# One-core perceiver layer pair: context turned by VectorE's block transposes, value products in fours, softmax maximum terms on GpSimd, ones rows by DMA

## The reference

```python
# layer 0: 4 heads of 64; mask of 128 x 12544; keys and values from one product
kv = (context @ Wkv)
attn = softmax(where(mask, q @ k.T * 64**-0.5, -inf))
out = attn @ v
...
# layer 1: 16 heads of 16, no mask
q = x_1 @ Wq.T + bq
k = x_2 @ Wk.T + bk
v = x_2 @ Wv.T + bv
out = softmax(q @ k.T * 16**-0.5) @ v
```

## Time and profile before

| | us |
|---|---|
| median of three runs (1105.54 to 1106.64) | 1106.38 |
| the profiled execution's own time | 1106.16 |
| its span in the trace | 1104.5 |
| PE busy | 1018.3 (92%) |
| DVE busy | 524.3 (47%) |
| ACT busy | 547.1 (50%) |
| POOL busy | 274.5 (25%) |

### The profile page before, as it was taken

The page is one execution under the profiler, slowest core; times in us unless marked ns, Lnnn a source line. Parts: engine busy times, 40 slices in busy tenths (PEclk is TensorE's granted clock), DMA queues, the critical chain, the costliest instruction groups (busy, mean ns, idle before and its releaser), DMA issues. The chain is left out here.

```text
span 1104.5 us, 22373 instructions
## 1 busy us (share of the span) xinstructions
PE 1018.3 (92%) x8536; PEld 587.8 (53%) x8536; DVE 524.3 (47%) x1094; ACT 547.1 (50%) x1252; POOL 274.5 (25%) x326
## 2 busy tenths in 40 slices
PE   7999999999999999999969987489999999999976
PEld 4445554554555455455457974125555555555653
DVE  2223232322323232232144443888878888787525
ACT  2544454454445445444547622116666666666752
POOL 4444253334425333442403610600000000000000
PEclk9999999999999999999989997559999999999988
DMA  4434625342363334233200006655556666555200
GB/s 146 155 140 170 232 95 194 118 159 84 113 228 116 135 117 163 83 109 131 104 35 1 1 1 186 177 139 139 140 142 175 169 171 178 139 140 152 67 1 6
DMA packets 65132, 136.79 MB, mean 124 GB/s; under 512 B 12584, under 2 KB 46912, under 8 KB 62368
## 3 DMA queue, kind: packets, MB, share of 16 engines
q1 hardware_dynamic: 65056, 135.72, 40.1%
HBM read 81.88 MB, written 53.26 MB: 122 GB/s over the span
## 5 line engine op out<-in xcount | busy, mean ns | idle before, releaser
L1724 DVE TENSOR_REDUCE mx<-bank 128x1 f32<-128x896 f32 x224 | 245.1, 1141 | 58.8 <-PE bank L1608 57.8
L1806 ACT ACTIVATE p<-bank 128x512 f32<-128x512 f32 x392 | 212.6, 595 | 115.7 <-PE bank L1651 114.9
L504 PE MATMUL bank<-Wv,ctxT 128*128 128x512 f32 x392 | 180.2, 600 | 0.0
L1608 PE MATMUL bank<-krows,qrows 96*128 96x512 bf16 x448 | 129.0, 377 | 27.4 <-DVE mx L1724 19.5
L1664 PE MATMUL bank<-p,v 128*32 128x128 f32 x3136 | 127.0, 279 | 5.5 <-ACT p L1806 5.1
L1651 PE MATMUL bank<-qrows,krows 99*128 99x128 bf16 x1568 | 122.6, 222 | 0.0
L577 DVE CUSTOM_DVE_ANT_0 sc<-bank,pen 128x448 f32<-128x448 f32 x112 | 65.7, 620 | 104.7 <-issue 104.7
L1664 PEld LDWEIGHTS bank<-p,v 128*32 128x32 f32 x3136 | 74.3, 109 | 71.6 <-issue 43.8
L1651 PEld LDWEIGHTS bank<-qrows,krows 99*128 99x128 bf16 x1568 | 89.1, 98 | 39.2 <-issue 35.7
L504 PEld LDWEIGHTS bank<-Wv,ctxT 128*128 128x128 f32 x392 | 70.1, 190 | 73.5 <-issue 72.5
L379 POOL CAST kt<-kf 128x512 bf16<-128x512 f32 (+1 forms) x56 | 31.1, 556 | 309.4 <-ACT kf L663 309.4
(11 more groups left out here) (287 smaller groups left out, 1263.2 us busy)
## 6 DMA issues: line engine op xcount, KB each, us to landing
krows<-kscr SPq DMA_DIRECT2D x14, 1536.0 KB, 10.2
krows<-kscr SPq DMA_DIRECT2D x14, 1152.0 KB, 11.4
vscr<-v1s SPq DMA_DIRECT2D x14, 1004.5 KB, 3.9
v<-vscr SPq DMA_DIRECT2D x14, 1004.5 KB, 11.1
ctx<-ctx SPq DMA_DIRECT2D x14, 896.0 KB, 6.4
kscr<-kt SPq DMA_DIRECT2D x14, 768.0 KB, 3.6
kscr<-kt SPq DMA_DIRECT2D x14, 576.0 KB, 3.0
kscr<-kt SPq DMA_DIRECT2D x14, 512.0 KB, 4.5
```

What stands on the lines that cost most here:

```text
L504: ins = pe.matmul(bank[kv_bank(op, s)][:], ctxT0[:, i, k * P:(k + 1) * P], Wv01[:, i].rearrange("p w o -> p (w o)"), start=(i == 0), stop= ...
L1608: ins = pe.matmul(bank[b + half][:, 0:HW[half]], qrows[0:KROWS, 0, h, :], krows[half][0:KROWS, r, krow(h), :], start=True, stop=True)
L1724: dve.tensor_reduce(mx1[:, c % 2, h:h + 1], psum[:, b:b + 2, :].rearrange("p b n -> p (b n)")[:, 0:CH], AX.X, ALU.max).then_inc(S("smread1 ...
L1806: act.activation(p1[:, g % PR, :], bank[ST1[g % 3]][:], ACT.Exp).then_inc(S("exp1"), 1)
```

## The change

Four things change. First, in layer 0 the context is no longer turned on PE. The load brings each row's 256 numbers as four pieces of 64 to the four blocks of 32 partitions (eight DMAs of 256-byte pieces a chunk in place of one of 1 KB pieces), so that DVE's transpose of 32 x 32 blocks, straight from `ctx0` to `ctxT0`, gives a turned context; the weights that meet it are loaded in the matching order of rows. Four DVE transposes of 448 columns replace 14 PE transposes and four DVE copies. The first chunk's load is issued by ACT. Two of the three weights of W are turned in the same way.

```diff
-        ctx0 = sb(l0, "ctx0", [P, 2, CT, D])
+        ctx0 = sb(l0, "ctx0", [P, 2, CH // SQ, QC])
...
+        def load_quarters(eng, tile, m, name):
+
+            rows = m.rearrange("(i t) d -> t i d", t=SQ)
+            for j in range(P // SQ):
+                eng.dma_start(tile[j * SQ:(j + 1) * SQ], rows[:, :, j * QC:(j + 1) * QC]).then_inc(S(name), 16)
+
+        def load_context(eng, c, s):
+            for half in range(2):
+                load_quarters(eng, ctx0[:, s, half * HG:(half + 1) * HG], ctx_rows[bass.ds(c * CH + half * HCH, HCH), :],
+                              f"ctx0_{s}_{half}")
...
                     if op[0] == "T":
-                        h, t0, nt = TG[k]
-                        dve.wait_ge(S("xp0"), 4 * c + k + 1)
-                        if some(NKV * c):
+                        half, i = k // 2, k % 2
+                        if i == 0:
+                            dve.wait_ge(S(f"ctx0_{s}_{half}"), 64 * n + 64)
+                        if k == 0 and some(NKV * c):
                             dve.wait_ge(S("kv0"), NKV * c)
-                        dve.tensor_copy(ctxT0[:, h, t0 * P:(t0 + nt) * P],
-                                        bank[SX[k % 2]][:, 0:nt * P]).then_inc(S("ctxT0"), 1)
+                        groups = slice(half * HG, (half + 1) * HG)
+                        dve.transpose(ctxT0[:, i, half * HCH:(half + 1) * HCH],
+                                      ctx0[:, s, groups, i * SQ:(i + 1) * SQ]).then_inc(S("ctxT0"), 1)
...
+                    elif op[0] == "W":
+                        dve.wait_ge(S("raw1_in"), 144)
+                        quarters = raw1.rearrange("p w c (i d) -> p w (c i) d", d=QC)
+                        for i in range(DC):
+                            for b in range(DC):
+                                dve.transpose(WTk[:, i, b * P:(b + 1) * P].rearrange("p (d h) -> p h d", d=D1),
+                                              quarters[:, 1, b * (P // SQ):(b + 1) * (P // SQ), i * SQ:(i + 1) * SQ]
+                                              ).then_inc(S("WT1"), 1)
+                            dve.transpose(Wv01[:, i, 1, :], quarters[:, 2, :, i * SQ:(i + 1) * SQ]).then_inc(S("WT1"), 1)
```

```diff
+            for half in range(2):
+                ones = krows[half][KROWS:KONES].rearrange("p s h m -> p (s h m)").rearrange("p (n m) -> p n m", m=P)
+                sp.dma_start(ones, bc(onesb[0:3, :], 1, [3, R1 * H1 * HW[half] // P, P])).then_inc(S("krows_ones"), 16)
...
         PLAN1 = (
-            ("S8",), ("S9", "R"), ("S10", "S11"), ("S12",), ("S13",), ("S14",), ("S15",),
-            ("S0",), ("M", "S1"), ("S2",), ("S3",), ("S4",), ("S5", "S6"), ("S7",))
...
+            (("S8",), ("S9",), ("R",)),
+            (("S10",), ("S11",), ("S12",)),
+            (("S13",), ("S14",), ("S15",)),
+            (("S0",), ("S1",), ()),
+            (("M",), ("S2",), ("S3",)),
+            (("S4",), ("S5",), ()),
+            (("S6",), ("S7",), ()))
...
+                def rescale(c):
+                    pool.wait_ge(S("acc1"), 2 * c + 1)
+                    pool.wait_ge(S("f1"), c + 1)
+                    pool.tensor_tensor(acc1[:], acc1[:], bc(f1[:, c % 2, :], 2, [P, H1, D1 + 1]), ALU.mult).then_inc(S("acc1"), 1)
...
-                pool.wait_ge(S("q3"), 3)
-                for half in range(2):
-                    pool.memset(krows[half][KROWS:KONES].rearrange("p s h m -> p (s h m)").bitcast(F32),
-                                TWO_ONES).then_inc(S("krows_ones"), 1)
-                    pool.wait_ge(S("krows_ones"), half + 1)
...
+                    for t in range(CT):
+                        for k in range(SLOTS):
+                            if k < 2:
+                                for u in (4 * t + 2 * k + 4, 4 * t + 2 * k + 5):
+                                    if u < UNITS:
+                                        scores(c, u)
+                                    elif c + 1 < NCH:
+                                        scores(c + 1, u - UNITS)
+                            else:
+                                for u in range(4 * t, 4 * t + 4):
+                                    values(c, u)
+                            for op in plan1(c, t, k):
+                                side(*op)
```

186 lines of the change are left out of this document (86 added, 100 removed).

## The result

The changed kernel takes 1065.5 us (median of four runs, 1064.24 to 1068.71; the kernel before beside it 1105.96). The ratio is 0.9641, 95% interval 0.9626 to 0.9656: 40 us gained, where I had forecast 61 and a time of 1045, and the time lies outside the range, which ended at 1063. The profiled execution of the changed kernel is the slowest of its four, 1068.71 us with a span of 1067.0.

A forecast was written before the change was run, and what follows sets the result against it. It took PE to bound layer 0 and layer 1's loop, and waits on DVE behind memsets to cost time at layer 1's start. 20.2 + 1.7 + 7.9 + 31.3 = 61.1 us off 1106.2 gave 1045 us, range 1035 to 1063.

The forecast's parts named there:

- Layer 0's border: Layer 0's 13 chunk borders: context transposes leave PE, gaining 1.55 us each, 20.2 us in all.
- the 8 us of that estimate: Layer 0: at 1.09 us a DVE transpose, K2 would wait about 0.6 us; total 8 us higher, 1053 us.
- The rival of two passes: Layer 0: DVE transposes cost 1.24 us or are held by POOL, losing 17 us; 1062 us, chance 0.11.
- Layer 0's prologue: Start of layer 0: PE loses 22 transposes, 2.9 us, and gets back a 1.2 us wait; gain 1.7 us.
- Ones by DMA: Layer 1's attention start: without memsets PE's third S starts 8.7 us sooner; 7.9 us after 0.8 off for M.
- Chunk 0: Layer 1's first chunk: a loop chunk's 2.5 us gain, less 0.8 for M waiting on POOL; 1.7 us.
- Layer 1's loop: Layer 1's attention: chunks go from 23.88 to 21.4 us; twelve gain 2.5 each, 30 us, 31.3 with the last two.
- 1.5 + 0.43 - 0.1: Per layer 1 chunk: changes into narrow products halved, 1.5 us; `read_out` bank wait gone, 0.43; fourth unit's bank costs 0.1.
- GpSimd's part: Per layer 1 chunk: PE's 0.62 us wait before the scores that follow M goes.
- The last two periods: Layer 1's last two chunks, with few or no S and held by ACT's exponentials, gain 1.3 us together.
- The rival on keys: Layer 1: a chunk's second gather lands after its 14.5 us, each microsecond over costing 11; 1078 us, chance 0.05.
- Layer 1 keeps its pace: Layer 1's loop: only waits of 1.05 us a chunk are won, 12 x 1.5 us less; 1063 us, chance 0.14.

The follow-up runs named there:

- e8: Changed kernel with chunk 0's context load issued by SyncE behind x, ahead of the query weights, instead of by ScalarE; 1070.9 us.
- e15: Changed kernel with memsets for the ones, late dec operations, eight DMAs a gather, and chunk 0's context loaded by SyncE behind the query weights; 1050.4 us.
- e13: Changed kernel with the ones by memsets behind the queries and three dec operations behind the prologue's maxima; start 9.0 us shorter, total as expected (1057 to 1058).
- e16: Kernel before with only the three dec operations moved behind the prologue's maxima; start 8.8 us shorter, total as expected (1097 us).
- e1: Changed kernel with the two ones DMAs issued behind chunk 0's gathers and values instead of ahead of them; 1072.2 us.
- e9: Changed kernel with the ones DMAs reading a row of ones in DRAM, 18 wide packets instead of 1008 of 256 B; 1065.5 us.
- e4: Changed kernel with key gathers of chunks 3 to 13 cut from 96 rows to 8; eleven loop periods 235.96 us against 244.38.
- e12: Changed kernel with gathers in 4 and 3 KB packets and layer 1's loop back in pairs, the maxima's terms staying on GpSimd; 1082.4 us.
- e5: Changed kernel with the ones written by GpSimd memsets in the stage before, behind its clears, instead of by DMA; 1068.7 us.
- e6: Changed kernel with the two ones DMAs issued by GpSimd through its own queue in the stage before, instead of by SyncE; 1067.9 us.
- e14: Changed kernel with memsets for the ones, late dec operations, and gathers in packets of 4 and 3 KB; 1054.7 us.

## Why the prediction was wrong, step by step

- **Layer 0's border: right.** 1.55 us a border forecast, (463.17 - 445.58) / 12 = 1.47 measured; the transpose 0.627 us for 0.62, the wait for `pT` 0.25 for 0.32, K2 never waited. The Trainium skill (VectorE: DVE Perf Modes, "The three transpose paths") has a figure for bf16 alone, from which I had scaled an estimate of 1.09 us; the trace has 0.627 for 448 columns of f32, so the 8 us of that estimate did not come. The rival of two passes, at 1062, happened to name nearly the time measured, by a mechanism that did not occur.
- **Layer 0's prologue: wrong, 1.7 forecast, about -0.6 measured.** One failing step is that ACT issues "eight once before it has anything to do", with "I cost this at nothing". ScalarE issued from 0.79 to 5.97, then loaded its table, and its hT copy came at 7.29 instead of 6.00; PE's next product started 1.3 us later. It had something to do at 6.00, and I had not looked up when. With the loads on SyncE the copy came at 6.13 (e8) and 6.08 (e15), though something else was late there. The other is that I priced the prologue at the upper clock: the K products took 1.8 us longer than before, seven or so at the lower level instead of three. How long it lasts varies: the first copy comes between 79.87 and 81.47 us in the thirteen traces in which ScalarE issues the loads, so the changed kernel's 80.91 is one draw of these.
- **Ones by DMA: wrong, 8.7 forecast for the start, -0.8 measured** (0.45 gained behind the queries' write, 1.3 lost in the stages ahead of it). The 8.7 us that the memsets cost were right (e13, e16). The failing step is that the two DMAs' "some ten microseconds to spare" would cover "even a slow transfer into three partitions". I costed the transfer's own lateness and not what stands behind it: SyncE's issuing (7.12 us for two gathers, 20.34 for the ones in e1), and at the end of it all the queries' write, 10.3 us for 2.3. How much of this is SyncE's issue and how much the slower transfers (e9) is not separated.
- **Chunk 0: 1.7 forecast, 0.0 measured.** M behind GpSimd was priced 0.8 and cost nothing: PE waits 1.73 there and waited 1.12 on VectorE before, but a wait of 0.66 behind it is gone, and from the third S to the first scores it is 24.74 us for 24.98. The 2.5 us of a chunk were lost mostly to the clock, a term that I had left out: 2 us by four microseconds more at 0.50. I had looked at the clock of the loop alone. What sets the place of the rise is open; in the traces with the changed loop this stretch takes 49.57 to 51.04 us.
- **Layer 1's loop: mechanism right, size wrong, 28.8 forecast for the 13 periods, 19.3 measured.** Every term of a chunk stood in e4. Its eleven periods gain 262.86 - 235.96 = 26.9 us, 2.45 each for my 2.5; 1.87 of it belongs to the fours (e12 against the quiet chunks) against my 1.5 + 0.43 - 0.1 = 1.83, and 0.6 to GpSimd's part against 0.62. The last two periods give 0.8 for 1.3. The missing 8.4 us are the stalls behind long key packets: this is the term that was mis-sized, "Twelve chunks give 12 x 2.5 = 30 us". The rival on keys asked only whether they land in time (they do: PE waits nowhere for `krows`), not what their transfers hold up. The kernel before had the same packets with a single stall of 0.16 us; its PE waited about 1 us a chunk anyway and used up its instructions about a tenth more slowly. Whether that spared it is not shown.
- **The rivals.** "Layer 1 keeps its pace" (0.14) came nearest in size, for another reason. GpSimd beside maxima was no danger. The Trainium skill (SBUF — State Buffer, "Who interferes with whom") has `tensor_reduce` free of contention with GpSimd on trn2. The trace of e13 agrees: 1.055 us for each of sixteen maxima, of which about nine ran beside the memsets.

The stages between layer 0 and the queries' write are 1.3 us longer in the profiled run of after; in e13 they are as before (137.4 us for 137.2), so I lay no weight on it.

## What to carry to other kernels

Ask of an added DMA three things, not one: when it lands, how long its issue keeps the issuing engine (and whether a block's border waits for that engine), and which small, urgent transfer stands behind its packets. Ask of an engine brought near 100% what arrives by the same roads as its data: once TensorE had no waits of its own, the length of other transfers' packets set its stalls, and cutting them in four gave back 6.8 us of 8.4. Ask of a stretch where an engine starts after idling which clock it gets: here about 2 us went twice. And before replacing an operation that disturbs a neighbour, look at which of the neighbour's operations it disturbs: here moving three tiny ones gave 8.8 us on the kernel before.

## What the runs showed of the hardware

- A memset on GpSimd of 3 partitions (18.16 us for two) holds VectorE's TENSOR_SCALAR of 8 columns for 7.16 and 7.80 us, and leaves TENSOR_REDUCE (1.055 us for 896 columns from PSUM in e13, 0.16 us for 8 in e5) and a TENSOR_TENSOR (0.17 us in e5) alone.
- 1008 packets of 256 B into three partitions, 0.037 us each, passed between 657.2 and 671.0 us in the changed kernel; an estimate from these numbers is that 1008 x 0.037 / 13.9 = 2.7 of the 16 DMA engines were at work on them. They kept SyncE issuing for 6.40 us there and for 20.34 us behind the gathers (e1). The same bytes in 18 packets were issued in 0.63 us (e9).
- The same bytes issued by GpSimd kept it from the end of its block until 674.64 us, 22.5 us behind the end of their issue (e6).
- Gathers in 16 KB packets stall a TensorE that has next to no other waits by 0.2 to 1.8 us at a time, in 4 KB packets by 0.2 to 0.7 us (once 1.3, in e14), at the same bytes; in 2 KB packets three stalls of 0.3 to 1.0 us were left in eleven chunks (e15).
- An f32 block transpose on VectorE of 448 columns takes 0.627 us, as long as a copy of the same width would by the 1.09 ns a column of the earlier trace rows used in the prediction.
- TensorE's upper clock comes back at no fixed distance behind the start of dense work: 4.7 to 9.0 us behind the first scores of layer 1's loop.
